# Attention phase of a transformer block: features drawn together before the values, and the scores of the next chunk first in their eighths

## The reference

```python
h = einsum('bhid,oi,od->bho', x, weighted_sum, weight)      # token mixing
a = layernorm(h)
hh = _ln(a, g1, beta1)
q = _phi((hh @ wq).reshape(b, s, H, DH), proj)              # phi(y) = elu(y @ proj) + 1
k = _phi((hh @ wk).reshape(b, s, H, DH), proj)
v = (hh @ wv).reshape(b, s, H, DH)
# scan over tokens: kv += k_t v_t^T ; ksum += k_t
#                   out_t = (q_t kv) / (q_t ksum + 1e-6)
a = a + outs.reshape(b, s, H * DH) @ wo
a = a + gelu(_ln(a, g2, beta2) @ w1 + b1) @ w2 + b2
h = h + a
h = h + moe_ffn(layernorm(h))                               # 8 experts and a shared one
```

## Time and profile before

| | us |
|---|---|
| median of 3 runs | 2528.15 (2528.08 to 2528.81) |
| profiled execution, its own time | 2524.87 |
| its span | 2523.1 |
| TensorE busy (share of the span) | 2212.0 (88%) |
| VectorE busy | 1784.6 (71%) |
| ScalarE busy | 1529.7 (61%) |
| GpSimd busy | 1469.6 (58%) |
| stretch 112 to 1545 (the 32 units): TensorE busy of 1433 | 1312.1 |

### The profile page before, as it was taken

The page is one execution under the profiler, slowest core; times in us unless marked ns, Lnnn a source line. Parts: engine busy times, 40 slices in busy tenths (PEclk is TensorE's granted clock), DMA queues, the critical chain, the costliest instruction groups (busy, mean ns, idle before and its releaser), DMA issues. The chain is left out here.

```text
span 2523.1 us, 64867 instructions
## 1 busy us (share of the span) xinstructions
PE 2212.0 (88%) x24112; PEld 1729.1 (69%) x24112; DVE 1784.6 (71%) x3983; ACT 1529.7 (61%) x2890; POOL 1469.6 (58%) x1449
## 2 busy tenths in 40 slices
PE   3799999999999999999989985899999999994764
PEld 2577777788777787778778874466666666662653
DVE  3477777777777777777777775478787888874443
ACT  3576777677766767677666664656565665651332
POOL 1466666666666667667666653045555565556676
PEclk8899999999999999999999998899999999997897
DMA  3344444444444434344344333011212121101775
GB/s 113 102 124 118 116 129 120 114 127 122 114 121 128 110 101 110 101 109 106 96 110 105 82 91 124 17 60 60 68 47 82 43 76 37 41 22 32 160 138 71
DMA packets 323207, 236.42 MB, mean 94 GB/s; under 512 B 40345, under 2 KB 288141, under 8 KB 322896
## 3 DMA queue, kind: packets, MB, share of 16 engines
q1 hardware_dynamic: 286640, 197.30, 28.8%
q0 software_dynamic: 23808, 21.74, 4.9%
q10 hardware_dynamic: 12448, 13.24, 1.7%
HBM read 73.32 MB, written 82.58 MB: 62 GB/s over the span
## 5 line engine op out<-in xcount | busy, mean ns | idle before, releaser
L964 POOL TENSOR_TENSOR lo<-z,hi 128x512 f16<-128x512 f32 x256 | 306.2, 1196 | 283.2 <-DVE hi L873 250.9
L1849 POOL DMA_INDIRECT slot_dram<-xt,slot_u x256 | 267.3, 1044 | 77.4 <-issue 77.4
L542 PE MATMUL pF<-nh,qk_h 128*128 128x256 f16 x1024 | 281.7, 275 | 8.4 <-DVE nl L861 4.4
L543 PE MATMUL pF<-nh,qk_l 128*128 128x256 f16 x1024 | 281.3, 275 | 0.0
L544 PE MATMUL pF<-nl,qk_h 128*128 128x256 f16 x1024 | 281.2, 275 | 0.0
L788 ACT ACTIVATE sh<-sm 128x512 f16<-128x512 f32 x256 | 160.0, 625 | 97.4 <-DVE sm L894 92.9
L976 POOL TENSOR_TENSOR ol<-on,oh 128x256 f16<-128x256 f32 x256 | 172.2, 673 | 60.6 <-ACT oh L811 60.6
L868 DVE SCALAR_TENSOR_TENSOR z<-pF,z 128x512 f32<-128x512 f32 x256 | 175.1, 684 | 21.4 <-ACT z L771 17.4
L983 POOL TENSOR_TENSOR kvl<-kvacc,kvh 128x260 f16<-128x260 f32 x192 | 157.8, 822 | 53.4 <-ACT kvh L819 53.4
L894 DVE TENSOR_TENSOR sm<-pS,mask 128x512 f32<-128x512 f32 x256 | 174.7, 682 | 17.4 <-PE pS L628 16.8
L542 PE MATMUL pO<-vh,sh 128*128 128x65 f16 x1024 | 120.1, 194 | 67.1 <-issue 47.8
(11 more groups left out here) (298 smaller groups left out, 8387.6 us busy)
## 6 DMA issues: line engine op xcount, KB each, us to landing
w_w<-in_x SPq DMA_DIRECT2D x128, 256.0 KB, 2.8
qdh<-hi SPq DMA_DIRECT2D x512, 64.0 KB, 2.1
qdl<-lo SPq DMA_DIRECT2D x512, 64.0 KB, 2.1
ks<-hi SPq DMA_DIRECT2D x256, 64.0 KB, 2.4
ks<-lo SPq DMA_DIRECT2D x256, 64.0 KB, 2.1
slot_dram<-blank ACTq DMA_DIRECT2D x8, 1360.0 KB, 6.6
xg<-slot_dram SPq DMA_DIRECT2D x40, 272.0 KB, 3.2
x_dram<-x SPq DMA_DIRECT2D x32, 256.0 KB, 2.4
```

Source lines behind the costliest of these rows:

```text
L542: pe.matmul(out, wh, mh, start=first, stop=False, skip_group_check=True)
L543: pe.matmul(out, wl, mh, start=False, stop=False, skip_group_check=True)
L964: nc.gpsimd.tensor_tensor(lo[:, n % 2, :, :], z[:, units(w, FEATS, n) % ZS, :, :], hi[:, n % MOVES, :, :], ALU.subtract).then_inc(fl_ready, 1)
L1849: nc.gpsimd.indirect_dma_start(io["slot_dram"], bass.IndirectOffsetOnAxis(slot_u[:, i % XT, c, k:k + 1], 0), xt[:, i % XT, c, :], None, bo ...
```

## The change

`DENSE` gets another order, and `unit` puts the scores elsewhere where g is 2 or 3. Before, the eighths 0 to 7 hold: f0 | f1, f2 | p, f3 | v0, v1 | f4 | f5, f6 | f7, v2 | v3. After: f0 | f1, f2 | p, f3 | f4, f5 | f6 | f7, v0 | v1, v2 | v3. In eighths 2, 3, 6 and 7 the `scores` of the next chunk now come before everything but the layer norm, and their `scores_split` right after the early product's `finish`. In eighths 0, 1, 4 and 5 only the dense products change. The prologue takes its features and values in the order of the same table.

```diff
--- before.py
+++ after.py
@@ -36,8 +36,8 @@
 FEAT_ORDER = (0, 4, 1, 5, 2, 6, 3, 7)
 
 
-DENSE = ((("f", 0),), (("f", 1), ("f", 2)), (("p", 0), ("f", 3)), (("v", 0), ("v", 1)), (("f", 4),),
-         (("f", 5), ("f", 6)), (("f", 7), ("v", 2)), (("v", 3),))
+DENSE = ((("f", 0),), (("f", 1), ("f", 2)), (("p", 0), ("f", 3)), (("f", 4), ("f", 5)), (("f", 6),),
+         (("f", 7), ("v", 0)), (("v", 1), ("v", 2)), (("v", 3),))
 LAST_BANK = 1
 TURNS = 6 * CH - 2
 AHEAD = 4
@@ -398,6 +398,9 @@
                     if s == 2 and real(ahead):
                         step("x0", ahead)
                         step("normed", ahead)
+
+                    if g >= 2 and quad is not None:
+                        step("scores", *quad)
                     for what in early:
                         use(u, *what)
                     step("outputs", i, c, g)
@@ -410,8 +413,10 @@
                         step("turn", i - 1, CH - 1, g + 2)
                     for what in early:
                         finish(u, *what[:2])
-                    if quad is not None:
+                    if g < 2:
                         step("scores", *quad)
+                    elif quad is not None:
+                        step("scores_split", *quad)
                     step("outputs_split", i, c, g)
                     if s == 1 and real(ahead):
                         step("var", ahead)
```

## The result

The changed kernel takes 2585.06 us (2580.64 to 2591.47) against 2528.11: a ratio of 1.0228, with an interval of 1.0204 to 1.0252. It is 57 us slower, where 25 were forecast; the range ended at 2582. The profiled execution took 2591.47 us.

A forecast was written before the change was run, and what follows sets the result against it. It took the chain from the projection's read through GpSimd and SP's issues to `kvl` as deciding: units 0.4 us longer, plus 0.4 for long issues, 0.8 over 31 units, 25 us on 2528: 2553 us, range 2521 to 2582.

The forecast's parts named there:

- the three waits: TensorE's attention-phase waits: pO's products on `sh` 47.8 us, scores for DMAs into `ks` 31.0, `sl` 16.2; 95 together.
- `kvl` in eighth 6: Expected sign: TensorE waits for GpSimd's `kvl` before eighth 6's outputs, 30 to 60 us in 31 places, from 2.9.
- GpSimd's `lo` for the moves of `qdl`: Expected sign: GpSimd's `lo` waits about 3 us per unit for DMAs of query features, near 100 us in all.
- the read of feature 4's bank: Expected sign: TensorE's pF waits for VectorE's `z`, 15 to 35 us in all.
- The first third: Start of a unit: without eighth 0's DMA wait, feature 2's pass and the layer norm come 0.8 us earlier.
- the mask: Eighth 2 on VectorE: the mask now precedes the division, so the projection's read slips by 0.6 us.
- issues from the load to feature 4's last move: SP's queue: 0.4 us for the load, 2.6 for feature 3's four moves, 4.5 to feature 4's last move.
- last issue to landing: From the issue of feature 4's last move until it lands, freeing the buffer feature 6 overwrites: 2.1 us.
- `lo` of feature 6 to the end of `kvl`: GpSimd after its DMA wait: `lo` 1.12, `ol` 0.63, `sl` 1.11, `kvl` 0.68; 3.5 us in all.
- outputs of eighth 6 to the next unit: End of a unit: 8.36 us before, less 0.45 for scores and 0.3 for an `sl` wait, gives 7.6.
- Rival 1: Feature 4's moves land in time: 0.4 to 1.5 us gained per unit, 2483 to 2515 us; chance 0.13.
- Rival 3: VectorE's and ScalarE's backlog delays eighth 5's mask, holding eighth 6's scores: 2569 to 2590 us; chance 0.13.

The follow-up runs named there:

- defer_lo6: The changed kernel, but GpSimd makes the low part of feature 6 only after eighth 4's `kvl`; 0.9988 of the kernel before.
- key_fourth: The changed kernel with a key feature moved up, so feature 4 is a key with four moves instead of a query with eight; 1.0013 of the kernel before.
- table_only: The kernel before with only the new `DENSE` table, the scores in their old places; 1.027 of the kernel before.
- defer_mask2: defer_lo6 with eighth 2's scores and splits back where they were before the change; 2513.87 us, 0.9929 of the kernel before.
- scores_only: The changed kernel with the old `DENSE` table, so only the scores are moved; 1.008 of the kernel before.

## Why the prediction was right about the way and wrong about the size

**The mechanism was right in each link.** What stood in place of the three waits was what the text named: `kvl` in eighth 6 (61.5 us, 30 to 60 expected), GpSimd's `lo` for the moves of `qdl` (108.2 us, near 100 expected), the read of feature 4's bank (26.2 us, 15 to 35 expected). defer_lo6 and key_fourth take one link each out, by different means, and each brings the time back to that of the kernel before, with ratios of 0.9988 and 1.0013. table_only shows that this part alone does it. (61.5 us is just above what was expected, and so are the units, 48.2 us in the mean of both kinds.)

**The first third and the mask: the place right, in part by luck.** The gain of 0.8 us by the earlier scores and the loss of 0.6 by the mask put the end of the projection's read at 20.2; the mean of second halves is 20.1. But that is also their mean before the change: the one unit that the sum started from had its read at 20.42, 0.3 later than the others. Without the mask ahead of it (table_only, defer_mask2) the read ends at 19.5 and 19.6. So the mask costs the 0.6 forecast, and the first third gains 0.5 in second halves, not 0.8.

**What was mis-sized** are four terms of the sum, each short, here in second halves against the unit of 46.2 us:

| term | as put | measured | short by |
|---|---|---|---|
| issues from the load to feature 4's last move: place of the last issue | 32.8, and 0.4 for long ones | 33.4 | 0.2 |
| last issue to landing | 2.1 | 2.7 | 0.6 |
| `lo` of feature 6 to the end of `kvl` | 3.5 | 4.0 | 0.5 |
| outputs of eighth 6 to the next unit | 7.6 | 8.4 | 0.8 |

The landing was taken from the profile page's median over all such moves. The last move of feature 4 isn't a median one: its mean was 2.7, with single ones of 3.2 to 3.6, and it was 2.5 already before the change. Why is open. The load of 256 KB behind it in the queue doesn't explain it: it follows within 0.7 to 0.9 us before the change too, and in scores_only and key_fourth, where the mean is 2.1 and 2.2.

In the unit shown `ol` is the 0.5: 1.11 us instead of 0.66. VectorE's `sl` beside it (577.04) took 1.19, where in the unit of the earlier trace rows it took 0.69:

```profile
727.92 0.69 DVE L901 TENSOR_TENSOR sl<-sm,sh 128x512 f16<-128x512 f32 x1
```

`sl` began while GpSimd's `lo` ran and ended 0.54 us after it; `ol` ended 0.52 us after `sl`. In each of the 25 units one of the four GpSimd instructions from `lo` to `kvl` began while VectorE's `sl` ran and took some 0.45 us longer; which of the four it is changes from unit to unit. SBUF — State Buffer, section "Summary: rules for kernel authors", of the Trainium skill says that when VectorE has two SBUF inputs while the GpSimd instruction reads SBUF, the second one to issue blocks until the first finishes. These rows agree: the one that began second was the longer one, by 0.45 to 0.5 us where the other had 0.6 left to run. The prediction had this rule, thought of VectorE's casts alone and dropped it, for the reason that TensorE waits for GpSimd by then anyway. The argument was upside down: just because TensorE waited for GpSimd, what slows GpSimd counts.

The 0.8 at the end is the clock: 1.7 us in nearly half of the second halves of the profiled execution; in the others it is 7.6 us from the outputs to the next unit, as put. The tail was copied from a unit in which TensorE had no long gap, and a gap of 1.5 to 3 us was the forecast itself (38.6 against 35.6 to 37.1).

Together 2.1 us more for second halves; the sum had +0.8 per unit, the traces show +3.2 for second halves (48.7 against 45.5) and +1.8 for first halves (47.7 against 45.9). The 0.3 that is left is the unit of 45.79, longer than the mean of its kind. In first halves the read ends at 19.0, 1.1 earlier than in second halves, and the chain with it; the prediction took the two kinds as one.

The units alone would make the loss larger than it is: the first 30 took 1434.5 us instead of 1364.6. From the last unit's start to the last output it was 67.3 instead of 73.1, and the first unit began 1.9 us later; the prediction had put both ends at 0 to 1 us. With half a microsecond behind the attention phase this makes 66.6 us between the two profiled executions, of which that of the changed kernel was the longest of its four (2591.47, median 2585.06) and that of the kernel before was 3.3 us under its median: so 57 between the medians.

**Rival 1** (in time after all) fell on its premise. DMA: Bandwidth & Descriptors, section "Issuing engines are not separate DMA queues", of the Trainium skill says that the time to initiate a DMA is usually small relative to the DMA itself; for moves of 64 KB issued one after the other it isn't here. It is 0.65 us each, against 2.1 to landing, and key_fourth's four issues are worth the whole loss. **Rival 3** (masks hold the scores of eighth 6) is there, but small: 8.8 us of waits, and they end before `kvl` does; in the unit shown the mask ended 35.9 us after the unit's start, as estimated. The measured 2585 lies in rival 3's 2569 to 2590, but not for its reason.

**What the prediction didn't see** is that the scores' part alone doesn't gain either. The text had put a gain of 0.4 to 1.5 us a unit on a kernel without GpSimd's wait; defer_lo6's units are 0.1 us longer than those before the change (45.8 against 45.7), and what it gains lies behind the last unit's start (66.5 us instead of 73.1).

## What to carry to other kernels

When an instruction is moved up on an in-order queue, ask what it waits for and list what is queued behind it: here a subtraction whose wait nobody noticed (its own result wasn't urgent) stood ahead of a small one that TensorE needed. A buffer that is freed by DMAs is freed by the queue that issues them, so count issues times their pitch, not only the time to landing. And where a forecast says that TensorE will stand idle for microseconds, the slower clock behind the gap belongs in the sum.

## What the runs showed of the hardware

- In one profile of the changed kernel 8 of 13 waits of 2.0 to 3.0 us in TensorE's work were followed by some 3.4 us at the lower clock level, 1.7 us lost each; 24 useless matmuls, 1.5 us in all, ahead of the wait removed that and made the kernel 10 us faster.
- SyncE issues a 64 KB move between SBUF tiles every 0.65 us; single issues take up to 2.1 us. Twelve of them stood ahead of the buffer that was needed; with eight (key_fourth) the loss was gone.
- A VectorE subtraction of 128x512 that began while a GpSimd one ran took 1.19 instead of 0.69 us, and the GpSimd subtraction of 128x256 that began while VectorE's ran took 1.11 instead of 0.66.
